# Attention similarities from rounded and low parts, with half of the key and query projections moved between the head couples

## The reference, cut to what matters

```python
q = x @ Wq
k, v = jnp.split(context @ Wkv, 2, axis=-1)      # heads: 16 of 64
sim = jnp.einsum('bhid,bhjd->bhij', q, k) * SCALE
sim = jnp.where(mask[:, None, None, :], sim, max_neg)
sim = jnp.clip(sim, -5.0, 5.0)
attn = jax.nn.softmax(sim, axis=-1)
out = jnp.einsum('bhij,bhjd->bhid', attn, v)
return out @ Wo + bo
```

## Time and profile before

| | |
|---|---|
| time, median of 3 runs | 1418.1 us (1417.98 to 1419.42) |
| the profiled execution | 1418.37 us, its span 1416.5 us |
| PE busy | 1334.9 us (94%) |
| DVE busy | 1096.4 us (77%) |
| ACT busy | 713.1 us (50%) |
| POOL busy | 724.0 us (51%) |
| chain that ended last | PE 79%, DVE 13% |

### The profile page before, as it was taken

How to read it: one execution, slowest core, us unless ns; L and a number is a source line. 1 busy time by engine, 2 the same in 40 slices (tenths; PEclk the granted TensorE clock), 3 DMA queues, 4 the chain that set the end, 5 groups by cost and what they waited for, 6 DMA issues and landing times.

```text
span 1416.5 us, 25256 instructions
## 1 busy us (share of the span) xinstructions
PE 1334.9 (94%) x9885; PEld 1003.6 (71%) x9885; DVE 1096.4 (77%) x1627; ACT 713.1 (50%) x1345; POOL 724.0 (51%) x1009
## 2 busy tenths in 40 slices
PE   9765699999999999999999999999999989998888
PEld 4443577777777787878686868686868667767765
DVE  1359998888888888888888888888888874344567
ACT  1353465555555546464646464656555534423455
POOL 0524446555555656464747474747474654340424
PEclk7878899999999999999999999999999999999999
DMA  9451212121212121212222222212222341030412
GB/s 372 163 183 36 80 42 76 52 72 53 72 53 72 53 72 53 72 53 72 63 69 69 58 73 61 72 53 72 57 62 52 82 146 31 1 105 2 152 39 83
DMA packets 57021, 109.85 MB, mean 78 GB/s; under 512 B 9422, under 2 KB 37574, under 8 KB 55750
## 3 DMA queue, kind: packets, MB, share of 16 engines
q1 hardware_dynamic: 39814, 61.64, 14.6%
q0 software_dynamic: 14848, 41.96, 10.4%
q10 hardware_dynamic: 2240, 4.63, 0.9%
HBM read 98.24 MB, written 9.95 MB: 76 GB/s over the span
## 4 chain that ended last, share of the span: by engine, by line
PE 79%; DVE 13%; issue 2%; another core or an unknown queue 2%; POOL 1%; DMA 1%; ACT 1%; SPq 0%; POOLq 0%; DVEq 0%
PE side_bank L379 48%; PE score_bank L379 28%; DVE cand_val L1108 3%; DVE cand_idx L1109 3%; PE score_bank L732 2%; DVE x_sum L1132 1%; DVE dispatchedT L1287 1%; DMA sc_in<-shared_compress 1%; PE side_bank L732 1%; POOL exp L1357 1%; DVE dispatchedT L1264 1%; POOL v_rows L1328 1%; PE side_bank L530 0%; PE score_bank L588 0%
## 5 line engine op out<-in xcount | busy, mean ns | idle before, releaser
L875 ACT COPY score_row<-score_bank 128x512 f32<-128x512 f32 x512 | 299.6, 590 | 170.4 <-PE score_bank L379 101.3
L1328 POOL DMA_INDIRECT v_rows<-in_V,top_idx x256 | 248.1, 969 | 188.6 <-DVE top_idx L1122 106.3
L1108 DVE MAX8 cand_val<-score_row 128x8 f32<-128x2048 f32 x128 | 291.8, 2280 | 57.8 <-ACT score_row L875 55.4
L1357 POOL TENSOR_SCALAR exp<-exp,exp_bound 128x256 f32<-128x256 f32 x512 | 243.7, 492 | 113.0 <-ACT exp L887 111.8
L1109 DVE FIND_INDEX8 cand_idx<-cand_val,score_row 128x8 uint32<-128x2048 f32 x128 | 292.5, 2285 | 0.0
L379 PE MATMUL score_bank<-keysT_hi,qT_hi 128*128 128x512 f32 x512 | 219.0, 428 | 31.1 <-ACT score_row L875 28.2
L379 PE MATMUL score_bank<-keysT_lo,qT_hi 128*128 128x512 f32 x512 | 205.2, 401 | 0.0
L379 PE MATMUL score_bank<-keysT_hi,qT_lo 128*128 128x512 f32 x512 | 204.8, 400 | 0.0
L887 ACT ACTIVATE exp<-side_bank 128x512 f32<-128x512 f32 x256 | 139.0, 595 | 98.5 <-PE side_bank L379 94.2
L379 PEld LDWEIGHTS score_bank<-keysT_hi,qT_hi 128*128 128x128 f32 x512 | 98.2, 192 | 70.1 <-ACT score_row L875 32.1
L379 PE MATMUL side_bank<-qT_heads,kT 64*128 64x256 f32 x1024 | 146.1, 404 | 1.0 <-ACT exp L887 0.8
(11 more groups left out here) (200 smaller groups left out, 2266.0 us busy)
## 6 DMA issues: line engine op xcount, KB each, us to landing
kT<-den_scratch SPq DMA_DIRECT2D x62, 256.0 KB, 4.3
f_quads<-in_f POOLq DMA_DIRECT2D x32, 256.0 KB, 3.5
comp_then_wqkv_raw<-in_comp SPq DMA_DIRECT2D x6, 1024.0 KB, 17.9
xT_by_step<-in_xTs SPq DMA_DIRECT2D x4, 1024.0 KB, 8.8
keysT_raw<-in_KmT ACTq DMA_DIRECT2D x8, 512.0 KB, 13.4
xT_in<-in_xT SPq DMA_DIRECT2D x16, 256.0 KB
x_sum<-in_x SPq DMA_DIRECT2D x32, 128.0 KB, 2.1
ctxT_in<-in_ctxT SPq DMA_DIRECT2D x16, 256.0 KB
```

Of the source, the lines that this page charges most:

```text
L875: nc.scalar.copy(srow[n // PER % 2][:, i * CB:(i + 1) * CB], scb[n % 3]).then_inc(sem("score_evac"), 1)
L1108: own(nc.vector.max(cv[:, tile, cs], srow[g % 2][:, :]))
L1328: pool.indirect_dma_start(out=vg[:, k, :], out_offset=None, in_=V_rows, in_offset=bass.IndirectOffsetOnAxis(ap=i8[:, tile, k:k + 1], axis=0))\
L1357: last = nc.gpsimd.tensor_scalar(ex[i % NEX][:, k, :], ex[i % NEX][:, k, :], ub[:, k, c:c + 1], E_LO, ALU.min, ALU.max)
```

## The change

`sims` multiplies three pairs of F32R parts. The keys are written to PSUM once and taken out by ACT twice: rounded (`khi`) and plain (`kraw_heads`); POOL subtracts (`keys_lo`). The queries are rounded by ACT (`qhi`), and DVE subtracts from the bank (`queries_lo`), which then frees the bank. K2, Q2 and K3, Q3 move into blocks 0 and 1, behind couples 1 and 3. The denominators are done per block, a quarter at a time, with six tiles of exponentials in place of ten. The rounding and low part of the next context move to after block 1 and head 9. `khi` lies on the memory of `kt`, `qhi` on that of `qt`, and `kraw_heads` on that of `klo`.

```diff
-NEX = 10
+NEX = 6
 def turn_jobs(c):
-        jobs += [("K", c, j) for j in range(4)]
+        jobs += [("K", c, 0), ("K", c, 1)]
     if out:
         jobs += [("WO", c - 1, t) for t in range(TT)]
     if cross:
-        jobs += [("Q", c, j) for j in range(4)]
+        jobs += [("Q", c, 0), ("Q", c, 1)]
     if prep:
         jobs += [("q", c + 3, 0)]
     if cross:
-        jobs += [("PV", c, j) for j in range(NP // 2)]
+        jobs += [("K", c, 2), ("Q", c, 2), ("PV", c, 0), ("K", c, 3), ("Q", c, 3), ("PV", c, 1), ("PV", c, 2), ("PV", c, 3)]
...
             def sims(c, p):
                 if p % 2 == 0:
-                    job_done(pe, ("K", c, p // 2))
+                    need(pe, "kT_lo", 4 * c + p // 2 + 1)
                     job_done(pe, ("Q", c, p // 2))
                 need(pe, "exp_done", H * c + 2 * p)
+                kl_, ql = klo[p // 2 % 2], qlo[p // 2 % 2]
                 for k in range(KT):
-                    for o in range(2):
-                        r = slice(64 * o, 64 * o + 64)
-                        last = mm(sp_[o][:, k * S:(k + 1) * S], kt[r, p, k * P:(k + 1) * P], qt[r, p, :])
+                    kc = slice(k * P, (k + 1) * P)
+                    for n, (left, right) in enumerate(((khi[:, p, kc], qhi[:, p, :]), (khi[:, p, kc], ql[:, p % 2, :]),
+                                                       (kl_[:, p % 2, kc], qhi[:, p, :]))):
+                        for o in range(2):
+                            r = slice(64 * o, 64 * o + 64)
+                            last = mm(sp_[o][:, k * S:(k + 1) * S], left[r, :], right[r, :], start=(n == 0), stop=(n == 2))
...
+            def denominators(c, j):
+                if j % 2 == 0:
+                    need(pe, "rden_done", 2 * c + j // 2)
+                for k in range(KT):
+                    for q in range(4):
+                        last = mm(den[32 * q:32 * q + 32, :], sel[:, j % 2, :], ex[(H * c + 4 * j + q) % NEX][:, k, :],
+                                  start=(j % 2 == 0 and k == 0), stop=(j % 2 == 1 and k == KT - 1))
...
-                for j in range(4):
+                for j in range(2):
                     if cross:
                         project(("K", c, j), 1, 2 * j * P, cth, ctl)
-                    score(c, j)
+                    score(c, 2 * j)
+                    score(c, 2 * j + 1)
...
-                for j in range(4):
-                    if cross and j == 3:
-                        sims(c, 0)
+                for j in range(2):
                     if cross:
                         project(("Q", c, j), 0, 2 * j * P, x1h, x1l)
                     score(c, 8 + j)
+                score(c, 10)
+                if cross:
+                    sims(c, 0)
                 if prep:
                     shared_q(a + 1)
+                score(c, 11)
                 for j in range(NP // 2):
...
                         values(c, j - 1)
-                        if j == 2:
-                            denominators(c, 0)
+                        denominators(c, j - 1)
                     if cross:
                         sims(c, 2 * j + 1)
                     select(c, 2 * j + 1)
+                    if cross and j < 2:
+                        project(("K", c, j + 2), 1, 2 * (j + 2) * P, cth, ctl)
+                        project(("Q", c, j + 2), 0, 2 * (j + 2) * P, x1h, x1l)
                     for e in range(4):
                         score(c, 12 + 4 * j + e)
... (ACT)
+            def keys_out(c, j):
+                key, ns = ("K", c, j), slice(2 * j, 2 * j + 2)
+                need(act, "ot_done", 2 * (c - 1) + 1 + j // 2)
+                job_full(act, key)
+                nc.scalar.copy(khi[:, ns, :].rearrange("p a s -> p (a s)"), job_bank(key)[:, :])
+                nc.scalar.copy(kraw_heads[j % 2][:, :, :].rearrange("p a s -> p (a s)"), job_bank(key)[:, :])\
+                    .then_inc(free(key), 1)
... (DVE)
+            def queries_lo(c, j):
+                key = ("Q", c, j)
+                need(dve, "heads_q_hi", 4 * c + j + 1)
+                if j >= 2:
+                    need(dve, "sim_full", NP * c + 2 * (j - 2) + 2)
+                nc.vector.tensor_tensor(qlo[j % 2][:, :, :].rearrange("p a s -> p (a s)"), job_bank(key)[:, :],
+                                        qhi[:, 2 * j:2 * j + 2, :].bitcast(F32).rearrange("p a s -> p (a s)"),
+                                        ALU.subtract).then_inc(free(key), 1)
...
-                candidates(c, 1)
+                candidates(c, 1, (0,))
+                queries_lo(c, 1)
...
-                candidates(c, 2)
                 if prep:
                     key = ("q", a + 1, 0)
...
+                candidates(c, 2, (2,))
...
                 candidates(c, 3)
                 select(c, (0, 1))
+                queries_lo(c, 3)
... (POOL)
+            def keys_lo(c, j):
+                job_done(pool, ("K", c, j))
+                nc.gpsimd.tensor_tensor(klo[j % 2][:, :, :], kraw_heads[j % 2][:, :, :],
+                                        khi[:, 2 * j:2 * j + 2, :].bitcast(F32), ALU.subtract).then_inc(sem("kT_lo"), 1)
...
                 if cross:
+                    keys_lo(c, 0)
+                    keys_lo(c, 1)
                     need(pool, "x1T_pe", TT * (c + 1))
...
+                    if cross and h in (3, 7):
+                        keys_lo(c, 2 + h // 4)
```

More of the change, by code:

```diff
@@ L202, in build @@
         cth, ctl = sb(work, "ctx_hi", [P, KT, S], F32R), sb(work, "ctx_lo", [P, KT, S], F32R)
+        split = work.enter_context(ExitStack())
+        khi = sb(split, "kT_hi", [P, NP, S], F32R)
+        qhi = sb(split, "qT_heads_hi", [P, NP, S], F32R)
+        kraw_heads = [sb(split, f"kT_raw{i}", [P, 2, S]) for i in range(2)]
+        split.close()
         kt = sb(work, "kT", [P, NP, S])
         qt = sb(work, "qT_heads", [P, NP, S])
+        klo = [sb(work, f"kT_lo{i}", [P, 2, S], F32R) for i in range(2)]
+        qlo = [sb(work, f"qT_heads_lo{i}", [P, 2, S], F32R) for i in range(2)]
         vv = sb(work, "v", [P, KT, INNER])
@@ L652, in _ @@
                     values(c, NP // 2 - 1)
-                    denominators(c, 1)
+                    denominators(c, NP // 2 - 1)
                 if mid:
@@ L904, in _ @@
                 cross, mid, prep = (0 <= b < B for b in (c, m, a + 1))
[L905 removed]
+                for j in range(2):
                     if cross:
[L907 to L909 removed]
+                        keys_out(c, j)
+                    score_out(c, 2 * j)
+                    score_out(c, 2 * j + 1)
                 for e in range(4, 8):
                     score_out(c, e)
[L912 to L914 removed]
+                for j in range(2):
                     if cross:
[L916 removed]
+                        queries_hi(c, j)
                     score_out(c, 8 + j)
[L918 to L919 removed]
+                if mid:
+                    weights8(m, 1)
+                score_out(c, 10)
+                if cross:
+                    exps(c, 0)
                 if prep:
@@ L932, in _ @@
                     select(c, 2 * j + 1)
+                    if cross and j < 2:
+                        keys_out(c, j + 2)
+                        queries_hi(c, j + 2)
                     for e in range(4):
@@ L937, in _ @@
                         weight_hi(2 * j + 1)
-                    if mid and j == 0:
+                    if mid and j == 1:
                         need(act, "ct_in", 16 * (m + 1))
@@ L1099, in own, with candidates @@
                 dve.wait_ge(sem("own"), n_own[0])
-            def candidates(c, s):
+            def candidates(c, s, between=()):
                 g = NCH * TT * c + 3 * NCH + AHEAD // PER + s
                 batch, tile, i = g // (NCH * TT), g // NCH % TT, g % NCH
-                if not 0 <= batch < B:
-                    return
-                cs = slice(8 * i, 8 * i + 8)
-                need(dve, "score_evac", PER * (g + 1))
-                own(nc.vector.max(cv[:, tile, cs], srow[g % 2][:, :]))
-                nc.vector.max_index(ci[:, tile, cs], cv[:, tile, cs], srow[g % 2][:, :]).then_inc(sem("cand_done"), 1)
+                cs = slice(8 * i, 8 * i + 8)
+                if 0 <= batch < B:
+                    need(dve, "score_evac", PER * (g + 1))
+                    own(nc.vector.max(cv[:, tile, cs], srow[g % 2][:, :]))
+                for j in between:
+                    queries_lo(c, j)
+                if 0 <= batch < B:
+                    nc.vector.max_index(ci[:, tile, cs], cv[:, tile, cs], srow[g % 2][:, :]).then_inc(sem("cand_done"), 1)
+            def queries_lo(c, j):
+                if not 0 <= c < B:
+                    return
+                key = ("Q", c, j)
+                need(dve, "heads_q_hi", 4 * c + j + 1)
[4 more added lines that the diff above has]
+                                        ALU.subtract).then_inc(free(key), 1)
             def merge(batch, tile):
@@ L1363, in _ @@
                         gather(m, 1, (6, 7))
```

(2 more changed lines are left out.)

17 lines of the change are left out of this document (7 added, 10 removed).

## The result

The changed kernel takes 1479.55 us (median of 4 runs, 1478.57 to 1480.63), the kernel before 1418.32 on the same chip: a ratio of 1.0428, interval 1.0412 to 1.0443, so 61 us more. The profiled execution has a span of 1477.6 us.

What follows compares the result with a forecast made beforehand. PE was taken as the bound, with DVE only 0.5 us behind in the first leg. A turn of 72.15 us, 3.6 more, gave 47 us over 13 turns, plus 11 elsewhere: 1476 us, range 1440 to 1495.

Steps and rivals of the forecast that it cites:

- Similarities: Couples on PE: 0.91 us each in place of 1.06, 1.2 us less a turn.
- rival C: Similarities on PE: the two heads do not run together in F32R, 1.63 us a couple, 1568 us; chance 0.05.
- K2 and K3 moved: Two projections, 2.85 us, leave PE's first leg for the second; the first leg gains nothing and becomes a wait.
- The first leg: K0 to Q0 in a regular turn: 17.8 + 1.8 = 19.6 us.
- DVE opens Q0 at 17.8: DVE's addition of WO0 frees Q0's bank 17.8 us into a turn and no sooner.
- the collision with the low parts: POOL's two key subtractions meet DVE's first weighted-sum operations: 1.8 us a turn, bounds 0 and 2.6.
- Rival B: First leg: no collision with POOL, 17.8 us, a turn 70.35, 1453 us in all; chance 0.26.
- The clock: PE's granted clock in regular turns: the forecast counted nothing for a fall.
- WO0 waits 1.1 us for POOL's product: First leg on PE: WO0, reached earlier, waits about 1.1 us for POOL, inside the wait for DVE.
- Rival D: Couple 0: a late report of its similarities costs 1 us a turn, 1490 us in all; chance 0.12.
- The others: Turns outside the regular ones: turn 0 +7, turn 14 +2, turn 15 +2, 11 us together.

Runs made afterwards that it cites:

- e8: Kernel before with products, low parts (heads 8 to 15's left out) and split denominators, projection order unchanged, first reciprocal ahead of candidates(c, 4): 1407.9 us, ratio 0.9923.
- e1: Kernel before with only the new projection order, similarities still float32, no low parts: 1435.9 us, ratio 1.0116.
- e5: Changed kernel with both keys_lo subtractions on POOL moved behind the addition of bo and rstd1: 1441.5 us, ratio 1.0153.
- e4: Changed kernel with five float32 filler matmuls on PE just before Q0, nothing removed: 1471.1 us, ratio 1.0366.
- e6: Changed kernel with queries_lo 2 and 3 placed later on DVE: 1474.0 us, ratio 1.0384.
- e9: Changed kernel with keys_lo and queries_lo 2, 3 later, residual2, queries_lo(c, 0), q's rounding and first reciprocal earlier, turn 0 reordered: 1420.2 us, ratio 1.0003.
- e3: Changed kernel with residual2 of tile 0 moved ahead of candidates(c, 0) on DVE: 1482.5 us, ratio 1.0447.
- e2: Kernel before with products, low parts (heads 8 to 15 reuse others') and denominators in four parts, projection order unchanged: 1435.4 us, ratio 1.0110.

## Why the prediction was right in sum, and where its steps were not

*Similarities.* 0.91 us a couple, as computed; two heads run side by side in F32R (rival C fell). e8 confirms the net of this and of the split denominators, 68.53 to 67.50.

*K2 and K3 moved.* Right in kind, and the main cause. The second leg is 52.74 us in a turn at full clock (70.65 - 17.91) against the 52.55 predicted, with the 0.43 us at the reciprocal against 0.4.

*The first leg: 19.6 predicted, 17.91 measured.* The step that failed is "DVE opens Q0 at 17.8", to which I added 1.8 for the collision with the low parts. e1 shows 16.26 for the leg without a collision, and e5 the collision at 1.66. So the size of the collision was near, and it was counted twice: the 17.8 had been read from a turn in which POOL's product already held the scaling (0.63) and `bo` the sum (0.79). The two subtractions put POOL back to where its late start had put it before. I had read the two operations of 0.91 and 0.84 us as a price list, and not as part of the number that I took for the floor. This is 1.7 x 13 = 22 us too much. Rival B, without a collision, came near the length of the turn at full clock (70.35 against 70.65) with a wrong reason: e5 shows that the collision is there, and what its absence brings is 69.0.

*The clock.* No step had it: its fall stood at nothing, without a reason. Eight falls behind the 2.28 us wait cost 11.5 us in the changed kernel, by e4 some 9 us net of the filler. The kernel before kept 1.00 in its regular turns, and none of my rivals had a fall of the clock in it.

*WO0 waits 1.1 us for POOL's product*: it did not (only in turn 15), as the product ended 2.6 us into the turn, and not 6.9 (658.47 - 651.57). *Rival D* fell: no late report stands behind couple 0 in any regular turn of the changed kernel.

*The others.* Turn 0 +7.5 (7 predicted), partly by the clock (0.93 granted in it, 1.00 before), so the agreement is in part luck. Turn 14 +9.5 (2 predicted): I had set the order on DVE there at nothing. PE waits 15.4 us in it, against 6.3. `queries_lo(c, 3)` waits for a projection, and the weighted sum and the logit behind it wait with it (8.09 us); e6 moves it and gets 4.7 us back. Most of the rest is Q0, which waits 5.09 us where it waited 1.84. Start and end of the run cost +5.5 against 2.

Altogether the regular turns gave 38.6 us (47 predicted) and the edges 22.4 (11 predicted). The floor that was set 22 us too high was made up for by the clock (11.5) and the edges (11), which is how 1476 came so near 1480: the mechanism was right in kind, and the last step from it to the number was luck. The gain of the products, 1.0 us a turn, was real; it was lost to an order on DVE and POOL that fitted the former legs, and e9 gets back 0.6 of it (7.8 us in 13 turns) without touching PE's list. Turns 0 and 14 (5.0 us) and the stretches outside of the turns keep e9 from ending below the kernel before; whether turn 14 can be mended as well was not tried.

## What to carry to other kernels

A floor read from another engine's timeline holds what that engine suffers in that turn: before something is added to it, strip it of the collisions of the same kind that it already holds. When work leaves a leg in which the second engine is half a microsecond behind, reorder the second engine in the same change: every addition that frees a bank, not the first alone (e3), and every operation that waits for a moved projection (e6). Two instructions at a bad place on POOL, which is busy for 54%, cost 38 us of 61 here, so move what nobody waits for behind the two-input work of its neighbour.

## What the hardware showed unexpectedly

An idle stretch of PE of 2.28 us between busy ones was followed, in eight turns of twelve, by a fall of the granted clock (0.58 from 695.05 to 698.50, between 1.00 and 1.00), and not in the other four. In the regular turns of e1, with 0.6 us of wait, and of e4, with the filler, the clock stayed at 1.00. What tells the two kinds of turn apart isn't settled.

A VectorE scaling of 128x8, 0.23 us alone, took 1.14 us beside a POOL subtraction and ended 0.03 us after it. In three places the hold was what was left of the POOL instruction, less some 0.2 us: 0.91 of 1.11 us here, 0.63 of 0.84 for the same scaling beside the product in the kernel before, and 0.43 of 0.63 for the first operation of the sum beside `bo`.

In the kernel before, the second reciprocal of turns 1 to 12 waited 3.9 to 4.5 us for something that the profile can't name and ran only 5.4 to 5.6 us ahead of K0. In the changed kernel, in e1 and in e2 it runs 8.71 us ahead, at the end of the denominators on PE, and its wait is named. Either half of the change makes the late report go away, so it isn't the split of the denominators alone; what held it stays open. It matters, since it set POOL's product, and with it the collision in the kernel before.
